# Even and odd time rows of the long convolution transformed apart in chunks 2 and 3, bias tables split once, and another order of pieces

## The reference, cut to what matters

```
xz = W_in x;  x, z = halves                    # 256 channels each
x  = silu(conv4(x) + conv_b)                   # short convolution, 4 taps
y  = irfft(rfft(x, 2L) * rfft(k_ssm, 2L))[:L]  # long convolution
y  = (y + x * D_skip) * silu(z)
out = W_out y
```

## Time and profile before

| | |
|---|---|
| time, median of 3 runs | 460.44 us (460.07 to 460.67) |
| the profiled execution: its own time | 460.52 us |
| its span, first to last instruction | 458.7 us |
| PE busy | 420.9 us, 92% |
| DVE busy | 330.3 us, 72% |
| ACT busy | 190.6 us, 42% |
| POOL busy | 21.8 us, 5% |
| mean granted clock of TensorE | 0.969 |

### The profile page before, as it was taken

The page is one execution under the profiler, slowest core; times in us unless marked ns, Lnnn a source line. Parts: engine busy times, 40 slices in busy tenths (PEclk is TensorE's granted clock), DMA queues, the critical chain, the costliest instruction groups (busy, mean ns, idle before and its releaser), DMA issues.

```text
span 458.7 us, 4175 instructions
## 1 busy us (share of the span) xinstructions
PE 420.9 (92%) x1398; PEld 211.1 (46%) x1398; DVE 330.3 (72%) x680; ACT 190.6 (42%) x314; POOL 21.8 (5%) x37
## 2 busy tenths in 40 slices
PE   4792987979999999999999999999999999999992
PEld 1341564655765365344644443433734433343361
DVE  4999898889973994597988674695553863274565
ACT  1343568443136412446143445344037526324441
POOL 0010203011000000000000000000000000000001
PEclk9896999979999999999999999999999999999997
DMA  6300000040000000000000000000000000000001
GB/s 220 150 1 0 1 1 0 2 149 2 1 0 1 1 0 0 1 0 1 1 1 0 1 0 23 0 1 1 0 1 0 24 0 1 1 0 0 1 0 46
DMA packets 5148, 7.27 MB, mean 16 GB/s; under 512 B 1075, under 2 KB 4232, under 8 KB 4872
## 3 DMA queue, kind: packets, MB, share of 16 engines
q1 hardware_dynamic: 3968, 4.80, 3.0%
q10 hardware_dynamic: 1160, 2.21, 1.4%
HBM read 5.95 MB, written 1.05 MB: 15 GB/s over the span
## 4 chain that ended last, share of the span: by engine, by line
PE 72%; DVE 6%; ACT 3%; issue 1%; POOL 1%; POOLq 0%; DVEq 0%
PE ring L1239 23%; PE ring L1217 8%; PE ring L1234 5%; PE timebank L274 5%; PE bankA L200 4%; PE ring L1219 4%; PE specbank L262 3%; PE ring L1247 3%; PE ring L1254 2%; PE ring L1258 2%; PE bankA L274 2%; PE ring L1261 2%; PE bankA L262 1%; PE ring L1265 1%; PE ring L1256 1%; PE ring L1262 1%
## 5 line engine op out<-in xcount | busy, mean ns | idle before, releaser
L1239 PE MATMUL ring<-hm,wc 128*128 128x512 f32 (+1 forms) x252 | 108.6, 581 | 0.0
L1239 PEld LDWEIGHTS ring<-hm,wc 128*128 128x128 f32 x252 | 46.1, 190 | 61.0 <-issue 52.8
L1445 DVE SCALAR_TENSOR_TENSOR hm<-xtm,cst,h 128x512 f32<-128x512 bf16 x48 | 33.4, 747 | 6.0 <-ACT h L1353 6.0
L200 PE MATMUL bankA<-wconv,h2w 128*128 128x256 f32 x128 | 34.9, 423 | 0.0
L1367 ACT ACTIVATE gts<-ring 128x512 f32<-128x512 f32 (+1 forms) x18 | 9.9, 550 | 52.3 <-PE ring L1239 52.3
L1353 ACT ACTIVATE h<-ring,vec 128x512 f32<-128x512 f32 x32 | 21.9, 687 | 17.0 <-PE ring L1219 14.9
L200 PEld LDWEIGHTS bankA<-wconv,h2w 128*128 128x128 f32 x128 | 25.7, 210 | 5.6 <-issue 2.0
L1534 DVE SCALAR_TENSOR_TENSOR f2e<-hl,f2e 128x512 f32<-128x512 f32 (+1 forms) x9 | 5.7, 632 | 27.2 <-ACT hl L1398 27.2
L1234 PE MATMUL ring<-hm,wc 64*128 64x512 f32 (+1 forms) x84 | 22.9, 621 | 0.4 <-DVE hm L1445 0.4
L1364 ACT ACT_TABLE_LOAD x8 | 10.3, 1283 | 28.4 <-PE ring L1239 28.4
L274 PE MATMUL timebank<-cst,abc 128*128 128x256 f32 x96 | 21.2, 379 | 0.0
(11 more groups left out here) (264 smaller groups left out, 762.5 us busy)
## 6 DMA issues: line engine op xcount, KB each, us to landing
wc<-in_w_c SPq DMA_DIRECT2D x1, 1664.0 KB
cst<-in_const ACTq DMA_DIRECT2D x1, 1096.0 KB
out<-xall SPq DMA_DIRECT2D x8, 128.0 KB, 1.9
wc<-in_x_feat SPq DMA_DIRECT2D x1, 768.0 KB, 13.0
bconv<-in_bcast SPq DMA_DIRECT2D x1, 512.0 KB, 7.6
wc<-in_k_time ACTq DMA_DIRECT2D x1, 512.0 KB
wc<-in_x_feat ACTq DMA_DIRECT2D x1, 256.0 KB, 3.7
wa<-in_w_a SPq DMA_DIRECT2D x1, 256.0 KB, 3.5
```

The source lines that it names most:

```text
L200: ins = pe.matmul(at, h2w[:, n, h * P + tap:h * P + tap + P], wconv[:, tap, :], start=False, stop=(h == HALVES - 1 and tap == TAPS - 1))
L1239: ins = pe.matmul(dst[:, at], wc[:, w:w + P], hm[:, seat(j, made + g - 1), at], start=False, stop=(g == PAIRS - 1))
L1445: dve.scalar_tensor_tensor(hm[:, seat(j, k), :], picked, cst[:, C_EG + g:C_EG + g + 1], h[:, g, :], ALU.is_equal, ALU.mult).then_inc(S["hm ...
```

## The change

**Folding.** With `FOLDED = UNFOLDED = (2, 3)`, chunks 2 and 3 no longer transform 256 time rows at once. The transform of the 128 even rows and that of the 128 odd rows are taken apart; for the even frequencies they are added, for the odd ones subtracted (`spectra`, two DVE instructions in PSUM, with the odd part copied to SBUF by ACT first, `keep_odd`). A half step is now one sequence b with both frequency parities, and no longer one parity of both sequences. A forward half is 4 calls with 256 columns. On the way back `products_now` ends with two further DVE instructions, and the inverse makes even and odd time rows from one pair of terms each: 16 calls with 128 columns for a chunk. Chunks 0 and 1 keep all terms: 8 calls with 256 columns for a forward half, 32 calls with 128 columns for an inverse.

**Layout.** `xtm` holds even rows, then odd rows, of each sequence, so `h2w` is written with even and odd columns apart, and `gate` reads `zs` and writes `ys` with a step of two. `const` shrinks from 2192 to 1677 columns.

**Bias tables.** One table `biases` of 88 rows and 384 columns holds `expert_b2` three times twice over and `conv_b` three times. It is loaded by one DMA on ACT's queue and split once at the start. The split of 24 rows in turn 4, the DMA on SP's queue that doubled it, and four small loads go. `ones` is a POOL memset.

**Order.** See the diff.

```
+FOLDED, UNFOLDED = (2, 3), (2, 3)
+        def forward_half(pe, c, b, bank, ahead=0):
+            after(pe, prod_done, 2 * c + b - ahead)
+            for e in range(2):
+                for ri in range(2):
+                    at = bank[:, e, ri * INNER:(ri + 1) * INNER]
+                    if c in FOLDED:
+                        ins = pe.matmul(at, block_of(C_FWD, e, 0, ri), xtm[:, c, b * HALVES + e, :], start=True, stop=True)
+                        continue
+                    for par in range(2):
+                        ins = pe.matmul(at, block_of(C_FWD, par, e, ri), xtm[:, c, b * HALVES + par, :], start=(par == 0), stop=(par == 1))
...
+        def keep_odd(act, c, b, bank):
+            if c not in FOLDED:
+                return
+            act.wait_ge(fwd_done, 2 * c + b + 1)
+            after(act, odd_used, folded(c, b) - 1)
+            act.activation(odd[:, :], bank[:, 1, :], ACT.Copy).then_inc(odd_kept, 1)
...
         def inverse_half(pe, c, cc, dst):
             pe.wait_ge(Z_ready, 4 * (c + 1))
+                for par in range(2):
+                    at = dst[:, (2 * b + par) * P:(2 * b + par + 1) * P]
+                    if c in UNFOLDED:
+                        for ri in range(2):
+                            ins = pe.matmul(at, z[:, par, ri, cols], block_of(C_INV, par, 0, ri), start=(ri == 0), stop=(ri == 1))
+                        continue
+                    for e in range(2):
+                        for ri in range(2):
+                            ins = pe.matmul(at, z[:, e, ri if c == 0 else 1 - ri, cols], block_of(C_INV, par, e, ri), ...)
...
+        def spectra(dve, c, b, bank):
+            dve.wait_ge(odd_kept, folded(c, b))
+            s.go(dve.tensor_tensor(bank[:, 1, :], bank[:, 0, :], odd[:, :], ALU.subtract))
+            dve.tensor_tensor(bank[:, 0, :], bank[:, 0, :], odd[:, :], ALU.add).then_inc(odd_used, 1)
...
         def products_now(dve, c, b, bank, between=None, ready=False):
+            whole = now
+            if c > 0:
+                whole = tt
+                s.go(dve.tensor_tensor(tt[:, :, 0, :], now[:, :, 0, :], last[:, :, 1, :], ALU.subtract))
+                s.link(dve.tensor_tensor(tt[:, :, 1, :], now[:, :, 1, :], last[:, :, 0, :], ALU.add))
+            dve.tensor_tensor(last[:, 0, :, :], whole[:, 0, :, :], whole[:, 1, :, :], ALU.add).then_inc(Z_ready, 1)
+            dve.tensor_tensor(last[:, 1, :, :], whole[:, 0, :, :], whole[:, 1, :, :], ALU.subtract).then_inc(Z_ready, 1)
...
 order (PE and ACT)
                 tail(0, "f1b")
+                forward(2, 0)
                 tail(0, "h1")
                 tail(0, "f2")
+                tail(0, "halt")
                 project_out(1)
-                tail(0, "halt")
-                forward(2, 0)
                 hiddens(1, 0, HU - 1)
                 turn(1)
+                shared(1, ALPHA)
                 hidden(1, HU - 1)
                 route_hidden(1)
                 beta(1)
                 logits(1)
+                forward(2, 1)
                 pair(1, ALPHA)
-                shared(1, ALPHA)
-                forward(2, 1)
...
                 turn(2)
+                route_hidden(2)
+                hiddens(3, 0, 2)
                 turn_back(1)
-                route_hidden(2)
-                hiddens(3)
+                hiddens(3, 2, HU)
...
                 tail(4, "f1b")
+                hiddens(5)
                 tail(4, "h1")
                 tail(4, "f2")
-                hiddens(5)
                 tail(4, "halt")
...
 DVE
                 gate(dve, 1, 1, Yb[1])
+                spectra(dve, 2, 0, Xb)
+                refine(0)
                 residual(dve, 1, Yb[0])
-                refine(0)
                 long_norm(dve, 1)
+                products_now(dve, 2, 0, Xb, ready=True)
                 masks_early(1)
                 masks_late(1)
-                products(dve, 2, 0, Xb)
+                products_late(dve, 2, 0, Xb)
                 pick(1)
                 post_beta(1)
-                products(dve, 2, 1, Xb)
+                products_now(dve, 2, 1, Xb)
                 post_alpha(1)
...
                 gate(dve, 2, 1, Yb[1])
-                post_beta(2)
+                products_late(dve, 2, 1, Xb)
                 residual(dve, 2, Yb[0])
                 long_norm(dve, 2)
                 refine(1)
+                post_beta(2)
                 products(dve, 3, 0, Xb)
                 pick(2)
```

More of the change, by code:

```diff
@@ L111, in constants @@
     c[:, C_E24] = EXPERTS - np.arange(P) % EXPERTS
[L112 to L117, removed]
+    c[:, C_RANK:C_ALL] = EXPERTS - np.arange(EXPERTS)
+    return c
 class Steps:
@@ L255, in two_layers @@
         bsteps = Steps(None, b_steps)
[L257 to L263, removed]
-            ins.then_inc(fwd_done, 1)
+        part = lambda c, b: abc[:, c % 3, :, :, b * INNER:(b + 1) * INNER]
@@ L285, in project_block @@
             ins.then_inc(out_done, 1)
[L287 to L293, removed]
+        taps = lambda d, ri: spec[:, :, ri, d, :]
@@ L300, in products_now @@
+        def products_now(dve, c, b, bank, between=None, ready=False):
+            s = bsteps
+            s.eng = dve
+            if not ready:
+                spectra(dve, c, b, bank)
+            xr, xi = real(bank), imag(bank)
+            now, last = part(c, b), part(c - 1, b)
+            after(dve, Z_ready, 2 * (2 * c + b))
+            after(dve, b_steps, s.base + s.n)
             if c == 0:
-                s.go(dve.tensor_tensor(both(now), x2(xr), taps2(e, 0), ALU.mult))
+                s.go(dve.tensor_tensor(now, x2(xr), taps2(0), ALU.mult))
@@ L302, in products_now @@
             else:
-                s.wait()
-                s.link(dve.tensor_tensor(both(tt[:, :, :]), x2(xr), taps2(e, 0), ALU.mult))
-                s.link(dve.tensor_tensor(now, now, tt[:, :, :], ALU.add))
-            s.go(dve.tensor_tensor(wide(tt[:, 0, :]), xi, taps(e, 0, 1), ALU.mult))
+                s.link(dve.tensor_tensor(tt[:, :, :, :], x2(xr), taps2(0), ALU.mult))
+                s.link(dve.tensor_tensor(now, now, tt[:, :, :, :], ALU.add))
+            s.go(dve.tensor_tensor(tt[:, :, 0, :], xi, taps(0, 1), ALU.mult))
@@ L327, in products_late @@
-        def products_late(dve, c, e, banks):
+            if c == 0 and c not in UNFOLDED:
+                dve.tensor_tensor(now[:, :, 0, :], now[:, :, 0, :], tt[:, :, 0, :], ALU.subtract).then_inc(Z_ready, 1)
+                dve.tensor_tensor(now[:, :, 1, :], now[:, :, 1, :], tt[:, :, 1, :], ALU.add).then_inc(Z_ready, 1)
+                return
+            s.go(dve.tensor_tensor(now[:, :, 0, :], now[:, :, 0, :], tt[:, :, 0, :], ALU.subtract))
+            s.link(dve.tensor_tensor(now[:, :, 1, :], now[:, :, 1, :], tt[:, :, 1, :], ALU.add))
@@ L719, in first_pool @@
                 pool.memset(neghalf[:, :], -0.5)
+                pool.memset(ones[:, :], 1.0)
                 pool.memset(der[:, DTOP:DTOP + 1], RATIO_TOP)
@@ L951, in two_layers @@
                 "picked gap_ready tg_ready full kept hm_ready xn_ready "
[L952 removed]
+                "refined y_turned c_var c_rstd out_ready out_sent oh_ready steps").split()}
             block = s2.enter_context(nc.Block())
@@ L1403, in _ @@
                 skip = lambda *key: None
-                order(turn, route_hidden, logits, spread, hidden, pair, shared, tail, last_pieces, skip, skip, skip, skip)
+                order(turn, route_hidden, logits, spread, hidden, pair, shared, tail, last_pieces, forward, skip, skip, skip)
             @block.vector
@@ L1670, in col @@
         return c
+    biases, masks = np.zeros((R_ALL, CTRL), np.float32), np.zeros((R_ALL, 3), np.float32)
+    for part in range(3):
+        for at in (part * EXPERTS, HID + part * EXPERTS):
+            biases[at:at + EXPERTS], masks[at:at + EXPERTS, part] = f["e_expert_b2"], 1.0
+        biases[R_CONV + part, 0:INNER], masks[R_CONV + part, part] = f["m_conv_b"].ravel(), 1.0
     vecs = np.concatenate([col(f["a_time_decay"]), col(f["a_time_first"]), col(f["a_time_mix_key"]), col(f["a_time_mix_value"]),
```

234 lines of the change are left out of this document (121 added, 113 removed).

## The result

The changed kernel takes 453.38 us, the median of 4 runs (452.55 to 453.85), beside 460.32 us for the kernel before on the same chip (460.07 to 460.67). The ratio is 0.9854, 95% interval 0.9839 to 0.9868: faster by 1.5%, 6.9 us. Forecast were 456.0 us with a range of 451.5 to 459.4. The side is right, the size is 2.6 us short.

The account below looks back on a forecast made before the run. PE was taken to bound the kernel, with DVE late from halt(1) to f1a(2). 2.15 + 1.7 + 3.35 - 0.2 - 0.2 = 6.8 us, less 2.4 for the clock, gave 460.44 - 4.4 = 456.0 us, range 451.5 to 459.4.

Parts of the forecast that it names:

- PE's savings: Folded forward halves save 1.70 us four times, folded inverses 3.35 twice, unfolded inverses lose 0.2 twice: net 13.1 us less.
- The rival of the narrow calls: At the four inverses, 128-column calls do not shrink, costing 0.38 us each: 468.8 us; chance 0.09, shared with longer DVE stretch.
- Steps 1 to 4: Walk from pair(0, GATE) to halt(1): waits of 0.45 us at hiddens(1), 1.5 at first mask; halt(1) ends 4.6 us earlier.
- Step 5: After halt(1), DVE works 22.1 us without a hole, f1a(2) starts at 264.6; post_beta(2) called in the worst spot.
- Steps 6 and 7: PE waits 3.0 us for pick, 1.3 for xn, keeping 2.15 at f1a(2); then chunk 3 folding gives 1.7 and 3.35.
- The clock's term: PE's wait at 258.4 brings the granted clock down, losing 2.4 us where PE binds again: 6.8 becomes 4.4.
- The clock holds: Rival: the clock does not fall at the stall of 258 to 265 us, giving 453.6 us; chance 0.28.
- chunk 0's inverse and small waits: Deductions in the walk's sum: 0.2 us for chunk 0's unfolded inverse, on the chain, and 0.2 for small waits.
- DVE is hidden after all: Rival: DVE work from 242 to 264.5 is 4.5 us shorter, all 13.1 us come through, 447.3 us; chance 0.05.
- two falls with 0.8 on top: Range's upper end, 459.4 us: clock falls also at 191 us (458.4, chance 0.12), plus a late first DMA of 0.8.
- Stage one: At the start, the larger bias split takes 3.9 us against 3.1, covered by DVE's 1.43 us wait: nothing or little.
- The step-two accesses: Gate and the h2w copy cost between nothing more and +0.7 us per instruction on the path; taken at nothing.

Follow-up runs that it names:

- nothing_folded: The changed kernel with no chunk folded, new order, layout, bias tables and narrow inverse calls kept: 462.5 us, 1.0061 of the kernel before.
- masks_first: The changed kernel with the 7 masks of job 1 put back ahead of products_now(2,0): 460.0 us, 1.0001 of the kernel before.
- post_beta_back: The changed kernel with post_beta(2) moved back ahead of residual(2): 455.72 us, 0.9909 of the kernel before.

## Why the prediction was right, and where its size was off

**PE's savings: right.** A folded half was put at 1.84 us and is 1.83; a folded inverse at 3.56 and is 3.67; an unfolded inverse at 7.12 and is 7.15. A 128-column call of these is 0.22 to 0.23 us. The page of the profile has 11.8 us less busy time against 13.1 forecast; it counts stretches at half clock in full. The rival of the narrow calls is out. The Trainium skill (TensorE: Matmul & The Clock Gate, Back-to-back issue gap) gives 81 ns a matmul at 128 columns against 131 at 512; these float32 calls do not follow that ratio. They went from 0.86 to 0.43 and 0.23 us as the columns were halved twice, with their weight loads beside them.

**Steps 1 to 4: right.** Halt(0) ended at 177.3 and `hiddens(1)` waited 0.34 us at 179.65, forecast 0.45 and 179.7. The wait at the first mask is 0.89 us at 192.38, forecast 1.5 at 192.5: the mask was on time, but PE's two calls on the bias rows (L1282, L1283), which the forecast left out of its gap, still ran up to 191.49. Halt(1) ends at 241.3, forecast 241.5.

**Step 5: right.** DVE's stretch is 22.1 us without a hole (242.12 to 264.18), as added up; f1a(2) starts at 264.32, forecast 264.6. Counted from halt(1), 1.45 us of DVE work put in moved f1a(2) by +1.65 us, 1.32 taken out by -1.33, and 2.66 taken out by -2.19, where PE's own work is the bound again: DVE binds there, shown, with 2.2 us to gain before PE does. What the step added in words was wrong. post_beta(2) is not in the worst spot; back at its old place the kernel is 2.3 us slower, since what it then holds up, `residual(2)` and the turn of chunk 2, leads to PE as well.

**Steps 6 and 7: right.** Waits of 3.0 and 1.3 us were forecast, 2.88 and 0.51 are seen; `spread(2)` between them took 2.7 us in place of 2, at a falling clock, so the sum is the same. Behind f1a(2) folding gives 5.2 us with the clock held (192.18 in nothing_folded less 186.97), forecast 1.7 + 3.35.

**The clock's term: right in kind, off in size.** This is the term that misses. 2.4 us were taken; 0.7 us were on the path (187.68 against 186.97 and 187.02). Of two stretches in the earlier trace rows the price was taken where dense work follows at once. Here the first 2 us of the fall lay under `spread(2)`, whose end nobody waited for while xn was not there. The two runs in which dense work follows the wait cost what was feared: about 2.8 us in masks_first, 3.0 in post_beta_back. So the forecast sum of 4.4 becomes 4.4 + 1.7 (clock) + 0.3 (f1a(2) at 264.32 and not 264.6) + 0.4 = 6.8, against 6.7 us between the two executions. The 0.4 is what the sum took off for chunk 0's inverse and small waits on top of the walk. That inverse did cost some 0.2 more, but PE came to it 0.38 us earlier (115.87 against 116.25), and whatever lies ahead of f1a(2) is in its start already.

**A rival had the number, not the reason.** *The clock holds* gave 453.6, much nearer to 453.38 than the forecast of 456.0. Its condition is false all the same: the clock fell in both executions of the changed kernel that were profiled. Its number is near because the fall cost little and the 0.4 above was not lost.

**Two side sums that do not come out.** *DVE is hidden after all* was to bring all 13.1 us with a shorter DVE stretch alone. By the walk's own numbers that gives 4.6 + 1.7 + 1.7 + 3.35 - 0.4 = 10.95, so 449.5; for 447.3 the waits at 179 and 191 us would have to go too. And two falls with 0.8 on top are 459.2, not the 459.4 of the range's upper end. Neither changes the forecast.

**Stage one: nothing, as forecast.** The split in the start runs from 6.48 to 10.36 us, 3.9 us, and DVE still waits 0.36 us for its first scan at 10.86, against 1.43 at 10.89.

```profile
6.48 0.35 DVE L822 CAST parts<-biasf 88x384 bf16<-88x384 f32 x1
...
10.86 1.39 DVE L854 TENSOR_TENSOR_SCAN mx<-der,mx,ksb 128x256 f32<-128x256 f32 x2 [0.36 <-ACT ksb L597]
```

The step-two accesses were bounded at 0.7 us each and taken at nothing. A gate operation is 683 ns in the mean and was 685; the `h2w` copies are 0.67 and 0.68 us and were 0.64. The Trainium skill (SBUF — State Buffer, the note on cachelines in the section on the DMA port swizzle) says that a stride of up to 4 float32 is free. The gate's 683 and 685 ns agree; the copies came out 0.03 us longer, for 520 elements in place of 518.

## What to carry to other kernels

Work taken off the bounding engine is won up to the point where the next engine is late, and that point can be added up beforehand: walk both lists side by side, here 22.1 us of DVE work without a hole. Once it is found, give back the saving exactly there, as leaving one of four forward halves whole did (1.3 us ahead of f1a(2), and the 0.7 us of clock behind it). Price a falling clock by what PE does while it is down: the same fall cost 0.7 us under waits and thin work, and 2.8 and 3.0 us in dense work.

## What the runs showed of the hardware

The same program with the same wait of 2.9 us lost its clock under `spread(2)` in one execution and from there into f1a(2) in another. The moment varies by some 2 us, and with it the time, by 0.7 us from f1a(2) to the end. The fall at the end of stage one varies as well: the clock stood at 0.50 or 0.53 in the three windows from 96 to 102 us in one of these executions, and at 0.66, 0.50 and 0.99 in the other. Waits that brought the clock down here were, in stage one, 2.49 us ahead of 77.64 and 1.25 with 1.40 two microseconds behind it, and then 2.88, 3.54, 4.17 and 4.34 us in one piece, and 1.82 with 0.78 behind it; after 1.09 alone, after 0.89, and after 0.32 and 1.17 with a filled stretch ahead, it stayed at 1.00. In masks_first it stood at 0.81 already in the window in which PE was idle.
